# Norm deviations in 64-token pieces, a router in column tiles, and the expert bias folded into the weights of a transformer block

## The reference

```python
def _ln_c(v, eps=1e-06):                       # over the 32 channels of a pixel
    return (v - mean(v, 1)) / sqrt(var(v, 1) + eps)
# attention: instance norm, qkv, 8x8 windows, 4 heads of 8 channels, projection
x = x + _L0_conv_ref(_ln_c(x), ...)
t = _to_tokens(x)                              # (8, 4096, 32)
def _L0_ffn_ref(x, router_w, router_b, expert_w, expert_b):
    router_probs = softmax(x @ router_w + router_b)          # 8 experts
    top_p, top_i = top_k(router_probs, 2)
    top_p = top_p / sum(top_p)
    expert_out = einsum('bnd,edc->bnec', x, expert_w) + expert_b
    return einsum('bnk,bnkc->bnc', top_p, take(expert_out, top_i))
t = t + _L0_ffn_ref(_ln_t(t), ...)             # _ln_t: the same norm, eps 1e-5
```

## Time and profile before

| | |
|---|---|
| median of 3 runs | 486.56 us (486.3 to 486.81) |
| the profiled execution | 487.85 us, its span 486.2 us |
| busy: PE, DVE, ACT, POOL | 402.4, 390.1, 242.5, 104.6 us |
| mean granted TensorE clock | 0.943 |
| first norm and first queries | 0 to 61 us |
| attention | 61 to 281 us |
| last attention chunk, norms of quads 0 and 1, gates of quad 0 | 281 to 331 us |
| mixtures 0, 1, 2, 3 | from 331.5, 372.7, 413.2, 451.2 us |

### The profile page before, as it was taken

How to read it: one execution, slowest core, us unless ns; L and a number is a source line. 1 busy time by engine, 2 the same in 40 slices (tenths; PEclk the granted TensorE clock), 3 DMA queues, 4 the chain that set the end, 5 groups by cost and what they waited for, 6 DMA issues and landing times.

```text
span 486.2 us, 12843 instructions
## 1 busy us (share of the span) xinstructions
PE 402.4 (83%) x4872; PEld 208.5 (43%) x4882; DVE 390.1 (80%) x511; ACT 242.5 (50%) x409; POOL 104.6 (22%) x152
## 2 busy tenths in 40 slices
PE   3786789999999999999999988469688698666863
PEld 1232346666666666666666543124234233111210
DVE  0389578999999999999999875976897997997643
ACT  3653367767777676677767670615323512102110
POOL 6730001011101110110111010003224324524632
PEclk9999779999999999999999998969899989879888
DMA  8400000000000000000000001932164737727541
GB/s 306 184 0 1 2 1 3 1 1 0 0 0 0 0 0 0 0 0 0 0 0 0 3 1 28 205 82 50 38 151 128 167 80 179 187 58 202 140 129 43
DMA packets 10901, 28.80 MB, mean 59 GB/s; under 512 B 3200, under 2 KB 4736, under 8 KB 10496
## 3 DMA queue, kind: packets, MB, share of 16 engines
q1 hardware_dynamic: 8400, 20.46, 16.6%
q0 software_dynamic: 2048, 6.29, 4.3%
q10 hardware_dynamic: 432, 1.77, 0.9%
HBM read 5.96 MB, written 4.19 MB: 21 GB/s over the span
## 4 chain that ended last, share of the span: by engine, by line
PE 45%; DVE 27%; issue 11%; ACT 6%; SPq 5%; DMA 2%; DVEq 1%; POOL 1%; POOLq 0%; ACTq 0%
PE psum L459 7%; DVE neg_max L927 6%; PE psum L321 5%; PE psum L476 5%; PE psum L341 4%; SPq L206 4%; PE psum L446 4%; PE psum L430 4%; DVE window_work L930 3%; PE psum L600 3%; PE psum L484 3%; PE psum L592 3%; PE psum L570 3%; DVE o_tok L938 2%; DVE rstd L363 2%
## 5 line engine op out<-in xcount | busy, mean ns | idle before, releaser
L728 ACT ACTIVATE probs<-psum 128x512 f32<-128x512 f32 x128 | 74.4, 594 | 25.1 <-PE psum L459 24.4
L930 DVE TENSOR_TENSOR window_work<-psum,neg_max 128x1024 f32<-128x1024 f32 x64 | 78.4, 1225 | 7.2
L927 DVE TENSOR_REDUCE neg_max<-psum 128x16 f32<-128x1024 f32 x64 | 77.0, 1203 | 7.3 <-PE psum L446 7.2
L459 PE MATMUL psum<-weights_sb,window_work 128*128 128x128 f32 x512 | 82.1, 283 | 0.9 <-ACT probs L728 0.9
L254 POOL TENSOR_TENSOR o_norm<-o_tok,o_rden 128x128 f32<-128x128 f32 x64 | 24.6, 406 | 249.8 <-DVE o_rden L940 249.8
L459 PEld LDWEIGHTS psum<-weights_sb,window_work 128*128 128x128 f32 x512 | 58.3, 142 | 43.5 <-issue 25.7
L476 PE MATMUL psum<-probs,v_cols 128*32 128x64 f32 x2048 | 55.4, 226 | 0.3 <-DVE o_tok L938 0.3
L592 PE MATMUL psum<-gate_rows,gate_sel_sb 128*128 128x512 bf16 (+1 forms) x118 | 42.3, 407 | 12.8 <-DVE window_work L1075 5.3
L1075 DVE TENSOR_TENSOR window_work<-stage,psum 128x512 f32<-128x512 f32 x48 | 31.8, 676 | 16.3 <-PE psum L592 10.9
L476 PEld LDWEIGHTS psum<-probs,v_cols 128*32 128x32 f32 x2048 | 34.6, 109 | 23.7 <-issue 20.6
L712 ACT ACTIVATE stage<-k_sb,weights_sb 128x512 f32<-128x512 f32 x64 | 44.3, 723 | 0.0
(11 more groups left out here) (95 smaller groups left out, 615.5 us busy)
## 6 DMA issues: line engine op xcount, KB each, us to landing
stage<-x_win SPq DMA_DIRECT2D x112, 128.0 KB, 2.6
out<-out_sb POOLq DMA_DIRECT2D x16, 256.0 KB, 2.5
stage<-in_x SPq DMA_DIRECT2D x3, 1024.0 KB, 14.4
stage<-x_win POOLq DMA_DIRECT2D x16, 128.0 KB, 3.7
gate_rows<-gate_parts SPq DMA_DIRECT2D x48, 32.0 KB, 1.8
stage<-in_x SPq DMA_DIRECT2D x2, 512.0 KB, 6.2
weights_sb<-weights ACTq DMA_DIRECT2D x1, 875.5 KB, 10.3
gate_f<-gate_sel ACTq DMA_DIRECT2D x1, 512.0 KB, 13.5
```

The lines of the kernel that those rows point to most:

```text
L459: last = nc.tensor.transpose(bank[TURN_BANKS[v % 2]][:, b * P:b * P + P], heads.rearrange("p h k -> p (h k)"), const["c_ident"][:, :])
L728: nc.scalar.activation(probs[:, w % 4, :], bank[TURN_BANKS[w % 2]][:, :], ACT.Exp).then_inc(exp_done, 1)
L927: nc.vector.tensor_reduce(m_t, t, AX.X, ALU.max, negate=True).then_inc(max_done, 1)
L930: nc.vector.tensor_tensor(shifted_unit[:, unit % 2, :, :, :], t, m_t.unsqueeze(3).to_broadcast([P, IMG, HEADS, TOK]), ALU.add).then_inc(sh ...
```

## The change

- **Deviations in pieces.** The eight equal copies of each variance row are used: the 512 tokens are cut in 8 pieces of 64, and 32 matmuls of 64 columns per quad (column tiles) accumulate piece r of each chunk into the rows of copy r. The deviation and reciprocal tiles are 64 columns wide instead of 512. The spread reads them with 32 matmuls whose weights are 32 rows by 128 columns, one for each piece and chunk (row tiles). In the first norm all spreads of a quad end together; in `next_norm` the spreads of chunks 0 and 1 take slots 11 to 14, those of 2 and 3 slots 15 to 18, each slot two pieces of two chunks, and the variance two slots.
- **Constants.** The weights of the pieces are made on the chip at the start, from memsets on POOL, small operations on DVE (`constants`) and eight bf16 matmuls; DVE copies 1024 columns out of PSUM. The first weight DMA is 163 columns instead of 675, and the first DMA of `x` one chunk instead of two.
- **Router** in four column tiles (32 output rows per chunk) in place of four accumulated matmuls; its halves take slots 20 and 21, after all four normalisations of the quad.
- **Expert bias.** `fold_experts` subtracts each image block's last weight row from the others and puts the bias there; after the router has read a quad, a DMA on SP (`last_channels`) sets the last channel of each image in `t_norm` to one. `bias`, `gate_f32` and one ACT copy go; the gate steps are 25. The repeats wait for this DMA.
- **Repeats on SP and ACT.** For quads 1 to 3, images 0 and 1 are copied by SP, 2 and 3 by ACT, four DMAs at a time, between its copies of the gates in chunks 0 and 2; POOL's are gone. For quad 0 SP issues all 32. SP then issues the ones of quad 1, and after that the first gate moves.
- The loops over quads outside attention are unrolled (SP, PE, ACT, DVE).

```diff
-            start = 2 * CHUNK
+            start = CHUNK
             sp.dma_start(stage[:, 0:start], x_v[0, :, 0:start]).then_inc(x_start_loaded, 16)
...
+            def last_channels(quad):
+
+                sp.wait_ge(logits_ps, quad + 1)
+                at = quad * (QUAD * CHUNK)
+                sp.dma_start(t_norm[C - 1:P:C, bass.ds(at, QUAD * CHUNK)].rearrange("p (j n) -> p j n", j=QUAD),
+                             ones[:, :].unsqueeze(1).to_broadcast([IMG, QUAD, CHUNK])).then_inc(last_set, 16)
...
             first = [j * CHUNK for j in range(QUAD)]
-            sp.wait_ge(ln2["normed"], QUAD + NORMED)
-            repeat_tokens(first[0], 0)
-            repeat_tokens(first[2], 1)
-            sp.wait_ge(filled, 4)
+            sp.wait_ge(filled, 5)
+            last_channels(0)
+            sp.wait_ge(last_set, 16)
+            repeat_tokens(first[0], 0, range(IMG))
+            repeat_tokens(first[2], 1, range(IMG))
+            last_channels(1)
             sp.wait_ge(gate_step, GATE_OPS + ONE)
             move_gates(first)
...
                 repeat_tokens(ats[2], 1)
+                if after:
+                    last_channels(q + 2)
...
+        def variances(pe, sems, quad, at=2, pieces=range(PIECES)):
+
+            if pieces[0] == 0:
+                pe.wait_ge(sems["std_ready"], quad + ONE)
+                pe.wait_ge(sems["squared"], quad * QUAD + (QUAD + XC))
+            for r in pieces:
+                for j in range(QUAD):
+                    last = nc.tensor.matmul(bank[at][32 * j:32 * j + 32, 0:PIECE], mean_pieces[r],
+                                            squares[:, j, r * PIECE:r * PIECE + PIECE],
+                                            start=(r == 0), stop=(r == PIECES - 1), skip_group_check=True)
+            if pieces[-1] == PIECES - 1:
+                last.then_inc(sems["var_ps"], 1)
+
+        def spread(pe, sems, quad, js, banks, source, pieces=range(PIECES)):
+
+            if pieces[0] == 0:
                 pe.wait_ge(sems["rstd_ready"], quad + (1 + ONE))
-            if half != 1:
-                pe.wait_ge(sems["normed"], c + (1 + NORMED - len(banks)))
-            one = nc.tensor.matmul(bank[banks[j % len(banks)]][:, cols(half)], const["c_spread"][:, j, :],
-                                   rstd[:, cols(half)] if rhs is None else rhs, start=True, stop=True)
-            if half != 0:
-                one.then_inc(sems["rstd_ps"], 1)
+                pe.wait_ge(sems["normed"], quad * QUAD + (js[-1] + 1 + NORMED - len(banks)))
+            for r in pieces:
+                for j in js:
+                    rows = slice(32 * j, 32 * j + 32)
+                    one = nc.tensor.matmul(bank[banks[j % len(banks)]][:, r * PIECE:r * PIECE + PIECE],
+                                           spread_pieces[rows, r, :], source[rows, :], start=True, stop=True)
+                    if r == PIECES - 1:
+                        one.then_inc(sems["rstd_ps"], 1)
...
-            nc.scalar.activation(std[:, :], bank[at][:, :], ACT.Sqrt, bias=eps).then_inc(sems["std_ready"], 1)
+            nc.scalar.activation(std[:, :], bank[at][:, 0:PIECE], ACT.Sqrt, bias=eps).then_inc(sems["std_ready"], 1)
...
-        LN1_BANKS, LN2_BANKS, LN2_FIRST = (3, 4, 5, 6), (3, 0, 1), (3, 4, 5)
+        LN1_BANKS, LN2_BANKS, LN2_FIRST = (3, 4, 5, 6), (3, 0, 1), (2, 3, 4, 5)
...
+            def constants(pe):
+
+                pe.wait_ge(const_step, 2)
+                for r in range(PIECES):
+                    last = nc.tensor.matmul(bank[3 + r // 4][:, r % 4 * P:r % 4 * P + P],
+                                            ident_pad[:, PIECES - r:PIECES - r + P], spread_one[:, :],
+                                            start=True, stop=True)
+                last.then_inc(spread_ps, 1)
+
+            def fold_experts(pe):
+
+                pe.wait_ge(const_step, 7)
+                nc.tensor.matmul(bank[7][:, 2 * C:4 * C], fold[:, :], const["c_we"].rearrange("p a n -> p (a n)"),
+                                 start=True, stop=False, skip_group_check=True)
+                for eh in range(2):
+                    nc.tensor.matmul(bank[7][:, (2 + eh) * C:(3 + eh) * C],
+                                     bias_sel[:, eh, :, :].rearrange("p i c -> p (i c)"), const["c_eb"][:, 0, 0:C],
+                                     start=False, stop=(eh == 1), skip_group_check=True)
...
+                    pe.wait_ge(mean_ready, 1)
                 variances(pe, ln1, q)
+            pe.wait_ge(spread_ready, 1)
...
-                    spread_first(q, j)
-                    centre(pe, ln1, q + 2, j, natural)
-                variances(pe, ln1, q + 2)
...
+                    centre(pe, ln1, q, j, natural)
+                    spread_first(q - 2, range(2 * j, 2 * j + 2))
+                variances(pe, ln1, q)
...
-                one = nc.tensor.matmul(bank[2][:, at], const["c_router"][:, j, :],
-                                       t_norm[:, bass.ds((quad * QUAD + j) * CHUNK + at.start, at.stop - at.start)],
-                                       start=(j == 0), stop=(j == QUAD - 1), skip_group_check=True)
-                if j == QUAD - 1 and half != 0:
+                for j in range(QUAD):
+                    start = (quad * QUAD + j) * CHUNK
+                    one = nc.tensor.matmul(bank[2][32 * j:32 * j + 32, at], const["c_router"][:, 0, 0:C],
+                                           t_norm[:, start + at.start:start + at.stop], start=True, stop=True)
+                if half != 0:
                     one.then_inc(logits_ps, 1)
...
+                if at in (8, 9):
+                    if at == 8:
+                        pe.wait_ge(gate_step, (quad - 1) * GATE_OPS + (1 + ONE))
+                    variances(pe, ln2, quad, pieces=range(4 * (at - 8), 4 * (at - 7)))
+                if 11 <= at < 19:
+                    js, part = ((0, 1), (2, 3))[(at - 11) // 4], (at - 11) % 4
+                    spread(pe, ln2, quad, js, LN2_BANKS, rstd, range(2 * part, 2 * part + 2))
+                if at in (20, 21):
+                    router(quad, half=at - 20)
...
-                        if k == 3:
-                            bias(quad, j)
...
+            def repeat_tokens(quad, pair, b):
+
+                act.wait_ge(y_step, (quad - 1) * 2 * QUAD + (4 * pair + 4 + Y))
+                act.wait_ge(last_set, quad * 16 + 16)
+                at = (quad * QUAD + 2 * pair) * CHUNK
+                for e in range(IMG):
+                    act.dma_start(x_rep[32 * e:32 * e + 32, pair, b, :, :].rearrange("p j n -> p (j n)"),
+                                  t_norm[32 * b:32 * b + 32, at:at + 2 * CHUNK]).then_inc(x_rep_act[pair], 16)
...
+                        if j == 0 and quad > 0:
+                            repeat_tokens(quad, 1, 2 + i)
+                        if j == 2 and quad + 1 < QUADS:
+                            repeat_tokens(quad + 1, 0, 2 + i)
```

189 lines of the change are left out of this document (103 added, 86 removed).

## The result

The change made the kernel slower: 497.21 us (median of four executions, 489.75 to 502.54) against 486.43 on the same chip, ratio 1.0133 (95% interval 1.0076 to 1.019). The forecast was 467. A ratio counts only the executions within 1.5 per cent of the fastest of their kernel (here 489.75 and 495.18), which is why it is smaller than the quotient of the medians.

What follows compares the result with a forecast made beforehand. DVE was taken to set the first three mixtures and to wait in the last, with the second norm's chain before them. Terms -0.8 - 5.3 - 4.3 - 3.0 - 2.5 - 4.3 = -20.2 gave 467 us, 8-in-10 range 457 to 479.

Steps and rivals of the forecast that it cites:

- mixtures 0 and 1, forecast at -7.3: First two mixtures: shorter DVE reciprocal (-2.75 each) and more PE slack; -4.3 and -3.0 us.
- I take 45: Norm's spread on PE: 45 ns for each of 64 records, 2.9 us against 3.45; bounds 1.0 and 9.3 us.
- Rival 2: Spread bound by its weight loads, 145 ns a record, 9.3 us per spread: slower, 501 us; chance 0.08.
- DVE's six operations 3.6, so I count no wait.: Mixtures 0 and 1: PE needs some 3.7 us from reciprocal to slot 14, DVE 3.6 before step 13's normalisation; no wait.
- I counted 1.4 us for it: Entry to the mixtures: +1.4 us for a clock that may fall while PE waits for the four normalisations.
- Entry, -5.3: 281 to 331 us: mixture starts at 326.1 instead of 331.49, with SP's queue late next; -5.3 us, from -7 to -3.
- First norm, -0.8: 0 to 61 us: +1.5 for new constants, -0.8 in each of the next two quads; sum -0.8, from -3 to +1.5.
- the 63 that I had named: Sign at the first attention reduction: expected at 60 to 61.5 us; later than 63 would make the first stage wrong.
- Router and bias, counted as slack for PE: Mixtures 0 and 1: PE loses four bias matmuls (4 x 0.86) and 2.4 of router; 5.4 us more slack.
- Mixture 2, -2.5: Third mixture: SP free at about 441, gate moves begin at 443.8, 0.5 to 1 us lost behind ACT's issues; -2.5 us.
- Rival 1: ACT's issues and full DMA engines eat the mixtures: 1 and 2 keep their length, 3 gains 2; 474 us, chance 0.23.
- Mixture 3, -4.3: Last mixture: about 1 us of DVE's 5.3 us wait for repeats remains, lost clock (1 us) comes back; -4.3 us.

Runs made afterwards that it cites:

- x0_after: The changed kernel run once more, nothing altered, as yardstick for other kernels on its chip: 492.07 us, ratio 1.0152 to the kernel before.
- n_four_oldq: Changed kernel with the spreads of all four chunks issued together over four row groups and repeats issued as before the change: 480.77 us, ratio 0.9878.
- j_four: Changed kernel with all four chunks' spreads issued together in slots 11 to 14, each chunk with its own PSUM bank: 487.77 us, ratio 1.0043.
- a_old_norm: Changed kernel with variance, deviation, reciprocal and spread back at full width, the rest of the change kept: 491.87 us, ratio 1.0126.
- the swap: SP moves the gates of quad 0 ahead of the ones of quad 1; alone on the changed kernel: 490.33 us, ratio 1.0062.
- the queues' experiment: Changed kernel with repeats back on SP and POOL, none on ACT: 495.42 us, no ratio; mixture 2 lasted 36.5 us.

## Why the prediction was wrong, step by step

By stretch, the profile of the changed kernel less that of before: first norm +2.4, attention -0.6, entry -1.1, mixtures +6.7, +7.4, +3.3, -3.4 (with the cuts of the earlier trace rows); sum +14.7 where -20.2 stood. The profile of `x0_after`, the same kernel at 491.56 us, gives +0.8, -0.6, -3.6, +3.1, +3.8, +3.5, -3.2; sum +3.7. In both the largest miss is mixtures 0 and 1, forecast at -7.3.

**The spread record, "I take 45".** This is the step that failed. At the upper level a record takes 31 ns when four row groups alternate (64 in 2.01 us at 293.17 in the entry) and 38 in a mixture of `n_four_oldq` (16 from 342.41 to the gate matmul at 343.02); with two row groups in turn eight take 0.59 us in `x0_after` (342.40 to 342.99), 74 ns, and 131 at the lower level. The norm of quad 1 in the entry shows it at one level (0.50), in `x0_after` in pairs and in `j_four` all at once:

```profile
310.80 3.67 PE L371 MATMUL psum<-rstd,spread_pieces 32*128 32x64 f32 x32 [3.30 <-DVE rstd L393]
317.26 3.68 PE L371 MATMUL psum<-rstd,spread_pieces 32*128 32x64 f32 x32 [2.79 <-DVE x_win L399]
```

```profile
311.24 3.69 PE L371 MATMUL psum<-rstd,spread_pieces 32*128 32x64 f32 x64 [3.30 <-DVE rstd L393]
```

The same 64 records take 7.35 us in pairs and 3.69 at once, and the 2.79 us between the pairs, a wait for a bank that DVE still had to read, go too. The estimate was good for quad 0 and wrong for every norm issued in pairs: the row it leaned on, 33 ns in the earlier trace rows, has weights of half as many columns.

Its argument was a clock misread. The prediction took 62 against 33 ns in the earlier trace rows as proof that row groups overlap, but the 62 ns row ran at the lower level. In the kernel before, the 62 and the 33 ns row; then the 62 ns row in `a_old_norm`:

```profile
51.67:53.58 1.91, 1.91 (x33) 1.79 (x33) 0.00 (x0) 1.91 (x4) 0.00 (x0) 0.50 0.04 9
281.54:283.17 1.63, 1.63 (x37) 1.01 (x36) 0.41 (x1) 1.08 (x2) 0.58 (x2) 1.00 0.00 0
```

```profile
51.76:52.84 1.08, 1.08 (x33) 1.01 (x33) 0.00 (x0) 1.08 (x2) 0.00 (x0) 1.00 0.00 0
```

At the upper level those 32 records take 34 ns each, as long as in the 33 ns row: its loads of 64 columns did not follow one another faster, and that was the reason for going down to 45. Twice the 34 ns for twice the weight columns, an estimate, is near the 74 measured in pairs.

Rival 2 named the right term and, with a chance of 0.08, nearly the right time (501), but the time is luck: it charged 145 ns throughout, and against the forecast +19 us in the first norm, +9.6 in the entry and +6 in mixtures 0 and 1, which in the profile came out 3.2, 4.2 and 21.4 us above the forecast.

**"DVE's six operations 3.6, so I count no wait."** The waits were 2.33 and 3.31 us in mixture 0, 2.68 and 3.31 in mixture 1. At 74 ns the first pair cost DVE little, 1.06 us in mixture 0 of `x0_after` and nothing in mixture 1. Its second pair came at the lower level again, and DVE waited 2.6 us for it in both:

```profile
346.93 0.69 DVE L399 TENSOR_TENSOR x_win<-x_win,psum 128x512 f32 x1 [1.06 <-PE psum L371]
...
354.64 0.69 DVE L399 TENSOR_TENSOR x_win<-x_win,psum 128x512 f32 x1 [2.63 <-PE psum L371]
```

`n_four_oldq` shows these waits gone, `j_four` all but 1.07 us in mixture 0.

**The clock.** I counted 1.4 us for it in the entry and none in the mixtures. In the profile of 502.54 us it fell to 0.50 at 346.8 us, after PE had stood 1.63 us for the reciprocal and run the first small matmuls, and stayed there until 370.6; in `x0_after` it fell at 349.1 and came back at 362.7. The kernel before falls there too (0.86 over its chunk 1) and comes back sooner. What decides how long it stays isn't settled: the two profiled executions of the changed kernel differ in it, and matmuls added to hold the clock cost more than they saved.

**Entry, -5.3.** Measured -1.1, and -3.6 in `x0_after`. The norm of quad 1 in two pairs at the lower level keeps PE until router 1, and SP, which had its repeats out at 323, waits for that router before it moves gates that are ready at 319.3. PE, DVE's last gate step, then SP's queue:

```profile
313.53 3.68 PE L371 MATMUL psum<-rstd,spread_pieces 32*128 32x64 f32 x32 [3.30 <-DVE rstd L393]
320.00 3.68 PE L371 MATMUL psum<-rstd,spread_pieces 32*128 32x64 f32 x32 [2.79 <-DVE x_win L399]
325.02 1.93 PE L620 MATMUL psum<-x_win,weights_sb 128*32 128x512 f32 x8 [1.34 <-DVE x_win L399]
```

```profile
318.56 0.69 DVE L1130 TENSOR_TENSOR gate_parts<-v_cols,gate_parts 128x512 bf16<-128x512 f32 x1 [0.70 <-ACT gate_parts L854]
```

```profile
301.87 21.09 SPq L223 DMA_DIRECT2D stage<-x_win  x32
327.01 0.61 SPq L230 DMA_DIRECT2D x_win<-ones  x1
327.67 7.55 SPq L216 DMA_DIRECT2D gate_rows<-gate_parts  x12
```

I had router 1 at about 322, covered by the repeats. In `n_four_oldq` the entry came to 44.3 us (-5.7), and with the swap as well to 42.2.

**First norm, -0.8.** Measured +2.4, and +0.8 in `x0_after`. The first reduction at 63.84 is past the 63 that I had named. The four variants with the full-width norm have it at 58.3 to 62.1, mean 60.6, the pieces in fifteen profiles at 62.0 to 64.5, mean 63.0: the pieces cost here too, about 2 us, though single executions overlap.

**Router and bias, counted as slack for PE.** PE's slack is worth nothing in a mixture that DVE sets. What counted was a step of DVE that I priced as "one ACT copy less" and didn't follow into the mixtures, where it moved another instruction into POOL's way: 1.2 us in each of mixtures 0 and 1. The 1.3 us that column tiles cost in chunk 2 don't show in the totals.

**Mixture 2, -2.5.** Measured +3.3. I charged ACT's issues "0.5 to 1 us"; they took 2.73 and 3.79 us for four each, 0.7 to 0.95 apiece, and the copy behind them held DVE 3.09 us. Another 3.78 us went to the gate matmul at 439.50, and by the queues' experiment all but 1.7 us of the mixture's loss goes when the old queues come back. Rival 1 named ACT's issues, but had mixture 2 keep its length, where it grew by 3.3, and mixture 3 gain only 2.

**Mixture 3, -4.3.** Nearly right: the wait for repeats fell to 1.91 us and the stretch by 3.4.

## What to carry over

Price a small matmul by a row with its own weight columns and its own number of row groups in turn, and read the granted clock of every row that you compare. Between two bounds nine times apart the guess needs a test of its own, and the order in which row groups alternate is part of the change. When an instruction is dropped from a hand-laced order, see what slides into its slot and which engine shares a port with it. Time taken from an engine that isn't the bound is worth nothing, and a second queue costs the engine that issues it its own work at that moment.

## What the runs showed of the hardware

- An f32 matmul record of 32 rows by 128 weight columns and 64 moving columns: 31 to 38 ns with four row groups in turn, 74 with two; at the lower clock level 58 (64 in 3.69 us) with four and 115 to 131 with two.
- The same kernel ran 489.75 to 502.54 us. By two profiles, 11 us apart, 7.6 us of the difference lie in two stretches in which PE stays at 1.2 GHz (0.50): each from 346.8 to 370.6 and 394.5 to 418.4 us in the one, 349.1 to 362.7 and 393.4 to 407.1 in the other.
- A VectorE subtraction with two SBUF inputs took 1.43 us instead of 0.69 when it met GpSimd's multiplication, and ended 0.56 us after it.
- Four repeats issued on ScalarE took 2.73 and 3.79 us, 0.68 to 0.95 each; on SyncE 0.64 to 0.77 (28 and 16 of them).
